# Edge search begun ahead of the small weights, its histogram counted in the same rounds, clears on two queues, last features split one group earlier

## The chip, the cores and the metric

One core of a Trainium2 chip. The metric is the device time of one execution in microseconds (us); the time before is the median of 3 runs. Engines: PE (TensorE), DVE (VectorE), ACT (ScalarE), POOL (GpSimd), SP (SyncE, which only issues DMAs here).

## What is computed

```python
edge_index = stack([src, dst])                       # 50000 edges, dst sorted, 3125 nodes, 256 features
# first layer, 3 hops:
msg = H[src...] * edge_weight                        # Hn = segment_sum(msg, rows) over the nodes
H = Hn @ Wn[i].T + bn[i] + H @ Ws[i].T + bs[i]       # elu after hops 0 and 1
x = layernorm(x + H)
# second layer, 8 heads of 32:
h = x @ W.T
alpha = leaky(h_src.a_src + h_dst.a_dst + sum(relu(edge_attr @ edge_W.T + edge_b) * h_dst))
attn = softmax of alpha over the edges of each dst
x = layernorm(x + segment_sum(h_src * attn, dst) + bias)
```

In the first layer `rows` is src and `cols` is dst.

## The kernel before, in words

The first layer multiplies by a dense adjacency of the graph that the kernel builds in HBM; the second works edge by edge on records sorted by dst. The kernel has these stages.

**Head.** SP loads edge ends, weights and attributes into tiles of 128 partitions x 392 edges (EC = 392), then the small weights (L444 to L449: b_cols, ew, a_cols, bias_b), x, and the weight matrices one after the other (L453, L467). Between the first matrix and the second stand 48 small copies of ew_parts into ew_j (L460, L463), which wait for parts that DVE makes in constants(). POOL clears the adjacency (10038528 words) with 18 DMAs of a zero tile, clear() at L411: 6 at once, 12 after some setup. DVE makes keys and cells of all edges in pair_cells(), and then the constants() that need the small weights.

**Search for equal pairs.** Two edges of one (dst, src) pair must be added up before they go to their cell. It runs in GROUPS = 49 rounds of U = 8 columns. For round t, DVE stages eight keys (kst, L1312), PE spreads them over all partitions (key_rows, L702), DVE compares them with the columns (find_pairs, L1323, eight compares of falling width, then to_cell L1327 and place L1330), PE adds the weights of equal pairs (pair_sums, L713, into a bank pair_totals(p)), and DVE reduces them to total (take_totals, L1334). POOL scatters each column with an adding indirect DMA (L578), 392 of them; it starts when all clears have landed, waits for the totals of each round, and for its own earlier scatters after each eight. In rounds 0 to 15 (UP = 16), PE takes four steps of first_products() after each round: transposes of the 7 weight matrices (L654), of x (L673), the first products (L643, L693). The other rounds are a hardware loop of two rounds per pass.

**Histogram of dst.** When the search is over, DVE splits the dst keys (L1353 to L1361, hi_d and lo_d), makes the one-hots of the window number, ohhi, for all 392 columns in seven instructions (L1372, over the tile of x_in), and then one low one-hot a round (ohlo, low_onehots, L1366) from which PE counts (count, L737, eight matmuls a round). Two ohlo buffers alternate. The histogram, copied at L1386, gives the start of each window's records.

**Ranks.** 49 rounds (PE rank_step L792, L799, spread L766, L777; ACT table copies; DVE ranks, L1426 to L1445) give the place of each edge in order of dst, place[:, 1].

**Hops.** SP waits for all scatters, places and table updates, then loads the adjacency in tiles a_t (L486). PE multiplies (L889) for 3 hops x 7 groups of 512 nodes (the last group, of 53, at L886), each over 25 windows. POOL meanwhile scatters the records by dst (L585), at times set by PE's progress, and reads them back (L590, s_dback). In hop 2 DVE does the layer norm of each group when its matmuls are done (L1513 residual, L1517, L1519, L1522), with means and variances on PE (L820, L826). Before the last group's residual, DVE calls split_features(), which splits the features of the records that were read back into three bf16 parts and makes the low keys (L1459 to L1477). PE then projects the last windows (L834), and the second layer begins.

The lines around the last split are these:

```python
for k in range(HOPS):
    for g in range(NG):
        if k == HOPS - 1 and g == NG - 1:
            split_features()
        ...
        if g < NG - 1:
            dve.wait_ge(s_amm, USED * (n + 1))
        else:
            dve.wait_ge(s_tail, 2 * HOPS)
```

Of the kernel before, what the change touches and what calls it, by code (L numbers as in the profile page):

```python
# [9 lines left out]
ALU = mybir.AluOpType  # L10
# [29 lines left out]
UP = 2 * U  # L40
# [43 lines left out]
def build(nc, x, src, dst, edge_attr, edge_weight, Wn, bn, Ws, bs, W, a_src, a_dst, edge_W, edge_b, bias, out):  # L84
    with ExitStack() as ctx:
# [88 lines left out]
        ohhiT = sb("ohhiT", [HI, U, P], F32, work)  # L174
        hist = sb("hist", [HI, LOK], F32, work)
# [78 lines left out]
        s_zero = sem("adjacency_cleared")  # L254
# [146 lines left out]
        def pair_totals(p):  # L401
            return bank[2 + p][:, 0:3 * U]
# [9 lines left out]
        def clear(eng, i):  # L412
            eng.dma_start(adj[i * P * FILL:(i + 1) * P * FILL, :].rearrange("(p c) o -> p (c o)", p=P),
                          zeros[:, :]).then_inc(s_zero, 16)
# [128 lines left out]
        def _(pool):  # L543
            pool.memset(identf[:, :], 0.0).then_inc(s_lane, 1)
            pool.wait_ge(s_blank, 5)
            for i in range(FILLS // 3):
                clear(pool, i)
# [17 lines left out]
            for i in range(FILLS // 3, FILLS):  # L565
                clear(pool, i)
# [3 lines left out]
            pool.wait_ge(s_zero, 16 * FILLS)  # L570
# [65 lines left out]
        def _(pe):  # L636
# [68 lines left out]
            def pair_sums(t, p, cold):  # L705
                pe.wait_ge(s_dup, U * t + U)
                if not cold:
                    pe.wait_ge(s_ptot, t - 1)
# [25 lines left out]
            def count(t, p, first, last=False):  # L734
                pe.wait_ge(s_lo, t + 1)
                for j in range(U):
                    i = pe.matmul(bank[1][0:HI, 0:LOK], ohhi[:, bass.ds(t * U + j, 1), :].rearrange("p c k -> p (c k)"),  # L737
                                  ohlo[:, p, j, :], start=first and j == 0, stop=last and j == U - 1, skip_group_check=True)
                i.then_inc(s_hist, 1)

            pe.wait_ge(s_hi, 7)
            pe.wait_ge(s_xT, len(ahead_x) + 2 * OWN_GROUPS)
            count(0, 0, True)
            count(1, 1, False)
            with pe.Fori(1, GROUPS // 2) as t:
                count(2 * t, 0, False)
                count(2 * t + 1, 1, False)
            count(GROUPS - 1, 0, False, True)
# [9 lines left out]
            def spread(t, s, n, cold):  # L758
                h, rows = bank[3 + s][0:HI, :], bank[5 + s]
                if cold:  # L760
                    pe.wait_ge(s_exc, 2)
                else:
# [251 lines left out]
        def _(act):  # L1014
# [8 lines left out]
            nc.scalar.copy(rec[:, 0:EC, 6], filled[:, :]).then_inc(s_rec, 1)  # L1023
            for m in range(2 * HOPS + 1):
# [10 lines left out]
            act.wait_ge(s_zero, 16 * FILLS)  # L1035
# [206 lines left out]
        def _(dve):  # L1242
# [66 lines left out]
            constants()  # L1309
# [31 lines left out]
            find_pairs(0, 0, True)  # L1341
            find_pairs(1, 1, True)
            take_totals(0, 0)
            with dve.Fori(1, GROUPS // 2) as t:
                find_pairs(2 * t, 0, False)
                take_totals(2 * t - 1, 1)
                find_pairs(2 * t + 1, 1, False)
                take_totals(2 * t, 0)
            find_pairs(GROUPS - 1, 0, False, True)
            take_totals(GROUPS - 2, 1)  # L1350
            take_totals(GROUPS - 1, 0)

            v.tensor_copy(dst_f[:, :], dst_i[:, :]).then_inc(s_hkey, 1)  # L1353
            v.tensor_scalar(cut_i[:, :], dst_i[:, :], SHIFT, None, ALU.logical_shift_right).then_inc(s_hkey, 1)
            v.tensor_scalar(group_i[:, :], dst_i[:, :], P - 1, None, ALU.bitwise_and).then_inc(s_hkey, 1)
# [430 lines left out]
```

## Time and profile before

| what | value |
|---|---|
| median of 3 runs | 3001.64 us (2999.54 to 3003.59) |
| the profiled execution, its own time | 3012.79 us |
| its span | 3011.0 us |
| mean granted TensorE clock | 0.786 |
| PE busy | 2305.8 us, 77% |
| POOL busy | 1634.0 us, 54% |
| DVE busy | 1471.4 us, 49% |
| ACT busy | 607.0 us, 20% |

The shares of busy time are means over stages with different limits. "Idle before" of a row is the time that its engine stood still before it, with what ended it. A line with an x count merges several instructions. Times of rows are microseconds from the start of the span.

### The profile page before, as it was taken

The page shows a single profiled execution, that of the slowest core. Times are in us where ns is not written, and L with a number is a line of the kernel's source. Part 1 is how long each engine was busy: PE and PEld are TensorE (multiplying, and loading weights), DVE is VectorE, ACT ScalarE, POOL GpSimd, SP SyncE. Part 2 cuts the span into 40 slices and gives each one's busy share as a digit, 9 for nine tenths or more (in the row PEclk, how much of TensorE's full clock was granted, in tenths as well). Part 3 has the DMA queues.
Part 4 walks back from the last instruction along what each step waited for, and adds up shares of the span by engine and source line. Part 5 has one row for each costly group of instructions (what it writes and reads, how often), then busy time and mean ns, then how long its engine had stood idle before and what let it go on. Part 6 is the DMA issues. An engine that isn't in the chain of part 4 may idle for free.

```text
span 3011.0 us, 40665 instructions
## 1 busy us (share of the span) xinstructions
PE 2305.8 (77%) x10293; PEld 1444.1 (48%) x10294; DVE 1471.4 (49%) x3883; ACT 607.0 (20%) x1667; POOL 1634.0 (54%) x1365
## 2 busy tenths in 40 slices
PE   0067443899999999999999999975566655664993
PEld 0055333577777644444444444444344443443772
DVE  2268999577777500000000111065565555667888
ACT  1021000022222100000001000012222222225994
POOL 1157777777777154444444442025555555545995
PEclk9987555555555699999999999987776677776997
DMA  9621221112121255444443445325555555554983
GB/s 382 239 22 1 0 0 0 0 1 0 0 0 0 69 148 144 131 116 139 133 136 108 136 131 163 113 81 169 171 156 165 161 163 162 164 155 143 270 267 113
DMA packets 297611, 350.47 MB, mean 116 GB/s; under 512 B 105434, under 2 KB 223921, under 8 KB 294961
## 3 DMA queue, kind: packets, MB, share of 16 engines
q1 hardware_dynamic: 205825, 247.70, 27.1%
q0 software_dynamic: 91696, 101.74, 16.5%
q8 instruction: 35, 0.57, 0.1%
q14 instruction: 55, 0.45, 0.0%
HBM read 242.39 MB, written 106.86 MB: 116 GB/s over the span
## 4 chain that ended last, share of the span: by engine, by line
PE 62%; issue 12%; DVE 11%; another core or an unknown queue 7%; SPq 4%; ACT 1%; DVEq 1%; DMA 0%; ACTq 0%; POOL 0%
PE psum L889 26%; PE psum L792 7%; PE psum L1006 7%; DVE found L1323 5%; PE psum L961 4%; PE psum L777 3%; SPq L447 2%; PE psum L799 2%; PE psum L737 2%; PE psum L643 2%; PE psum L878 2%; PE psum L766 1%; PE psum L952 1%; DVE acc L1557 1%
## 5 line engine op out<-in xcount | busy, mean ns | idle before, releaser
L578 POOL DMA_INDIRECT adjacency<-total,place x392 | 613.4, 1565 | 336.7 <-DVE total L1334 139.8
L585 POOL DMA_INDIRECT rows_by_dst<-rec,place x392 | 376.7, 961 | 501.4 <-PE psum L889 475.5
L599 POOL DMA_INDIRECT gath<-gat_rows,rec x416 | 398.5, 958 | 450.0 <-ACT digits L1186 183.3
L889 PE MATMUL psum<-a_t,acc 128*128 128x512 f32 x1200 | 527.1, 594 | 4.7 <-DMA a_t<-adjacency 4.7
L889 PEld LDWEIGHTS psum<-a_t,acc 128*128 128x128 f32 x1200 | 228.6, 191 | 275.3 <-issue 272.6
L961 PE MATMUL psum<-x,acc 128*128 x832 | 298.2, 510 | 65.7 <-DVE acc L1557 48.8
L1323 DVE SCALAR_TENSOR_TENSOR found<-psum,key_f,not_before 128x1024 bf16<-128x1024 f32 (+7 forms) x392 | 293.2, 815 | 0.1
L889 PE MATMUL psum<-a_t,x 128*128 128x512 f32 x600 | 262.2, 592 | 0.0
L961 PEld LDWEIGHTS psum<-x,acc 128*128 128x128 f32 x832 | 199.5, 257 | 130.2 <-issue 90.5
L1557 DVE TENSOR_TENSOR acc<-wT,psum 128x528 f32<-128x528 f32 x208 | 145.7, 700 | 220.4 <-issue 168.6
L792 PE MATMUL psum<-table,ohhiT 32*128 32x128 f32 x784 | 238.9, 457 | 0.3 <-ACT table L1065 0.3
L1006 PE MATMUL psum<-ht 128*128 128x264 f32 x832 | 210.8, 401 | 3.6 <-ACT ht L1214 3.6
L1498 DVE TENSOR_SCALAR et<-et 128x512 f32<-128x512 f32 (+1 forms) x28 | 11.6, 416 | 410.3 <-ACT et L1106 266.7
L615 POOL TENSOR_TENSOR ht<-gath,digits 128x1024 f32<-128x1024 f32 x104 | 198.1, 1913 | 18.1 <-ACT digits L1202 7.7
L792 PEld LDWEIGHTS psum<-table,ohhiT 32*128 32x128 f32 x784 | 181.1, 318 | 39.0 <-issue 21.6
L1169 ACT ACTIVATE wT<-psum 128x512 f32<-128x512 f32 x208 | 114.5, 596 | 418.8 <-remote 279.8
L1006 PEld LDWEIGHTS psum<-ht 128*128 128x128 f32 x832 | 152.4, 192 | 61.8 <-DVE x L1690 32.2
L702 PE MATMUL psum<-identf,kst 128*128 128x128 f32 x392 | 85.5, 392 | 124.7 <-DVE kst L1312 120.4
L889 PEld LDWEIGHTS psum<-a_t,x 128*128 128x128 f32 x600 | 113.9, 190 | 134.1 <-issue 133.0
L713 PE MATMUL psum<-w_parts,found 128*128 (+1 forms) x1764 | 59.9, 167 | 150.0 <-DVE found L1323 150.0
L928 PE MATMUL psum<-identb,lo_b 128*128 128x128 bf16 x420 | 64.1, 252 | 112.8 <-issue 81.0
L1426 DVE SCALAR_TENSOR_TENSOR terms<-psum,dst_f,earlier 128x128 f32<-128x128 f32 (+1 forms) x392 | 140.0, 414 | 10.9 <-DVE rank L1438 7.9
(282 smaller groups left out, 3018.2 us busy)
## 6 DMA issues: line engine op xcount, KB each, us to landing
a_t<-adjacency SPq DMA_DIRECT2D x450, 256.0 KB
gat_h_by_edge<-gath SPq DMA_DIRECT2D x104, 528.0 KB
gath<-gat_h_by_edge SPq DMA_DIRECT2D x104, 528.0 KB, 4.5
adjacency<-zeros POOLq DMA_DIRECT2D x18, 2178.5 KB, 48.3
gath<-gat_rows,rec POOLq DMA_INDIRECT x416
adjacency<-total,place POOLq DMA_INDIRECT x392
rows_by_dst<-rec,place POOLq DMA_INDIRECT x392
x_in<-in_x SPq DMA_DIRECT2D x1, 3072.0 KB
```

Source lines behind the costliest of these rows:

```text
L578: pool.indirect_dma_start(out=adj, in_=total[:, c:c + 1], out_offset=bass.IndirectOffsetOnAxis(ap=place[:, 0, c:c + 1], axis=0), in_offset ...
L585: pool.indirect_dma_start(out=rows_dst, in_=rec[:, c, :], out_offset=bass.IndirectOffsetOnAxis(ap=place[:, 1, c:c + 1], axis=0), in_offset ...
L599: pool.indirect_dma_start(out=gath[:, g % 4, c % 4, :], out_offset=None, in_=hh_dram, in_offset=bass.IndirectOffsetOnAxis(ap=rec_i[:, c, 0 ...
L615: nc.gpsimd.tensor_tensor(val[:, q, :, 0:D].rearrange("p c (h d) -> p c h d", h=HEADS), gath[:, q, :, 0:HX].rearrange("p c (h d) -> p c h ...
L792: pe.matmul(bank[7 * s][:, j * LOK:(j + 1) * LOK], ohhiT[:, 4 * s + j, :], table[:, half, :], start=True, stop=True, skip_group_check=True ...
L889: i = pe.matmul(sums[b], table_g[:, w, b * P:(b + 1) * P], a_t[:, q % NA, 0:width(g)], start=k == 0 and g < OWN_GROUPS and w == 0, stop=w ...
L961: i = pe.matmul(bank[4 + j][:, 0:HX], ohT[:, q % 2, j * P:(j + 1) * P], x0[:, bass.ds(ws[4 * (q % 2) + j], 1), :].rearrange("p c k -> p (c ...
L1006: pe.matmul(bank[4 * (q % 2) + j][:, 0:HX], onehot[:, q // 2, 4 * (q % 2) + j, :], val[:, q, j, :], start=True, stop=True).then_inc(s_mm, 1)
L1169: nc.scalar.activation(er[:, q % 2, 2 * p:2 * p + 2, :].rearrange("p c (h d) -> p (c h) d", d=HW)[:, :, 0:HD], bank[2 + p].rearrange("p (a ...
L1323: v.scalar_tensor_tensor(out=found[:, p, found_at(j):found_at(j) + n], in0=pair_rows(p)[:, j * P:U * P], scalar=key_f[:, bass.ds(t * U + j ...
L1426: v.scalar_tensor_tensor(out=terms[:, j, 0:wide], in0=bank[5 + q][:, j // 2 * 2 * P:j // 2 * 2 * P + wide], scalar=dst_f[:, bass.ds(t * U ...
L1557: v.tensor_tensor(prod[:, q % 2, 2 * p:2 * p + 2, :], er[:, q % 2, 2 * p:2 * p + 2, :], psum[:, (4 + 2 * p) * 512:(6 + 2 * p) * 512] .rear ...
```

## The change

- pair_cells() is followed at once by the split of the dst keys and by the first two rounds of the search; constants() comes after them.
- Each round of the search also makes a low one-hot (as before) and a window one-hot for its eight columns (the new tile ohhi_t, two buffers), and PE counts them after pair_sums, into bank 2. pair_totals has one bank instead of two, so pair_sums(t) waits for the totals of round t - 1 (before: t - 2). The seven ohhi instructions remain after the search, and the separate loop of the histogram is gone.
- first_products() is taken up in rounds 2 to 17 (UP = 18).
- 12 of the 18 clears are issued by ACT, after its copies into rec, with a semaphore of their own; POOL issues the first 6.
- split_features() is called one group sooner, before the residual of the last group but one.

```diff
-UP = 2 * U
+UP = 18
+        ohhi_t = sb("ohhi_t", [P, 2, U, HI], BF16, work)
         def pair_totals(p):
-            return bank[2 + p][:, 0:3 * U]
+            return bank[3][:, 0:3 * U]
# POOL
-            for i in range(FILLS // 3, FILLS):
-                clear(pool, i)
...
-            pool.wait_ge(s_zero, 16 * FILLS)
+            pool.wait_ge(s_zero, 16 * (FILLS // 3))
+            pool.wait_ge(s_zero2, 16 * (FILLS - FILLS // 3))
# ACT, after the copies into rec
+            act.wait_ge(s_blank, 5)
+            for i in range(FILLS // 3, FILLS):
+                clear(act, i, s_zero2)
# PE, pair_sums
                 if not cold:
-                    pe.wait_ge(s_ptot, t - 1)
+                    pe.wait_ge(s_ptot, t)
# PE
+            def count(t, p, first=False, last=False):
+                pe.wait_ge(s_lo, t + 1)
+                for j in range(U):
+                    i = pe.matmul(bank[2][0:HI, 0:LOK], ohhi_t[:, p, j, :], ohlo[:, p, j, :], start=first and j == 0,
+                                  stop=last and j == U - 1, skip_group_check=True)
+                i.then_inc(s_hist, 1)
             for t in range(UP):
                 key_rows(t + 1, (t + 1) % 2, t == 0)
-                pair_sums(t, t % 2, t < 2)
-                for _ in range(4):
-                    next(products, None)
+                pair_sums(t, t % 2, t == 0)
+                count(t, t % 2, t == 0)
+                if t >= 2:
+                    for _ in range(4):
+                        next(products, None)
...
-            with pe.Fori(U, GROUPS // 2) as t:
+            with pe.Fori(UP // 2, GROUPS // 2) as t:
                 key_rows(2 * t + 1, 1, False)
                 pair_sums(2 * t, 0, False)
+                count(2 * t, 0)
                 key_rows(2 * t + 2, 0, False)
                 pair_sums(2 * t + 1, 1, False)
+                count(2 * t + 1, 1)
             pair_sums(GROUPS - 1, 0, False)
+            count(GROUPS - 1, 0, False, True)
# DVE
             pair_cells()
-            constants()
+            v.tensor_copy(dst_f[:, :], dst_i[:, :]).then_inc(s_hkey, 1)
...
+            def count_onehots(t, p, cold):
+                if not cold:
+                    dve.wait_ge(s_hist, t - 1)
+                v.tensor_tensor(ohhi_t[:, p, :, :].rearrange("p c (a b) -> p c a b", b=2),
+                                hi_d[:, bass.ds(t * U, U), :].unsqueeze(2).broadcast_to([P, U, HI // 2, 2]),
+                                pairs_of(iota_b[:, 0:HI]).unsqueeze(1).broadcast_to([P, U, HI // 2, 2]),
+                                ALU.is_equal).then_inc(s_hi, 1)
+                low_onehots(t, p)
...
             find_pairs(0, 0, True)
+            count_onehots(0, 0, True)
             find_pairs(1, 1, True)
             take_totals(0, 0)
+            count_onehots(1, 1, True)
+            constants()
             with dve.Fori(1, GROUPS // 2) as t:
                 find_pairs(2 * t, 0, False)
                 take_totals(2 * t - 1, 1)
+                count_onehots(2 * t, 0, False)
...
             find_pairs(GROUPS - 1, 0, False, True)
             take_totals(GROUPS - 2, 1)
+            count_onehots(GROUPS - 1, 0, False)
             take_totals(GROUPS - 1, 0)
...
+            dve.wait_ge(s_hist, GROUPS)
             for c in range(0, EC, EC // 7):
...
-                    if k == HOPS - 1 and g == NG - 1:
+                    if k == HOPS - 1 and g == NG - 2:
                         split_features()
```

## Rows read from the trace of the kernel before

**Rows 1.** Busy time by stage: stretch, length, each engine, clock, DMA share, GB/s.

```profile
60.00:108.00 48.00, 0.00 (x0) 0.00 (x0) 0.00 (x0) 0.00 (x0) 0.00 (x0) 1.00 1.01 428
281.00:520.00 239.00, 105.00 (x1480) 90.56 (x1480) 218.66 (x666) 0.00 (x0) 180.08 (x117) 0.50 0.20 0
603.00:1027.00 424.00, 423.66 (x2343) 322.02 (x2341) 332.79 (x1219) 105.72 (x293) 279.38 (x179) 0.50 0.18 0
```

**Rows 2.** DMA issues of the page (first), then the timeline of the head: start, duration.

```profile
adjacency<-zeros POOLq DMA_DIRECT2D x18, 2178.5 KB, 48.3
...
24.81 0.49 DVE L380 CAST w_parts<-w_in 128x392 bf16<-128x392 f32 x1
...
46.52 63.98 SPq L447 DMA_DIRECT2D a_cols<-in_L_gnn_a_dst  x1
...
116.91 0.17 DVE L1294 TENSOR_TENSOR bcol<-b_cols 128x6 f32<-128x6 f32 x1 [90.94 <-DMA bias_b<-in_L_gnn_bias]
```

**Rows 3.** Timeline from 150 to 185 us: the stall for the second weight matrix.

```profile
156.92 1.11 PE L654 MATMUL psum<-identf,wraw 128*128 128x128 f32 x4 [26.57 <-DMA wraw<-in_L_gnn_Ws]
...
167.54 0.17 DVE L1312 COPY kst<-key_f 128x8 f32 x1 [32.51 <-PE psum L702]
...
183.41 0.21 DVE L1312 COPY kst<-key_f 128x8 f32 x1 [8.98 <-issue]
```

**Rows 4.** Timeline of the search: one round on PE, and to_cell of rounds 21 and 48.

```profile
317.88 1.33 PE L713 MATMUL psum<-w_parts,found 128*128 x36 [3.92 <-DVE found L1323]
...
319.10 1.97 PE L702 MATMUL psum<-identf,kst 128*128 128x128 f32 x8
...
324.69 0.17 DVE L1327 SCALAR_TENSOR_TENSOR to_cell<-left,cell 128x8 f32<-128x8 f32 x1
...
518.60 0.17 DVE L1327 SCALAR_TENSOR_TENSOR to_cell<-left,cell 128x8 f32<-128x8 f32 x1
```

**Rows 5.** Timeline of the keys, the window one-hots and the histogram.

```profile
520.35 0.35 DVE L1353 CAST dst_f<-dst_i 128x392 f32<-128x392 int32 x1
...
522.72 7.10 DVE L1372 TENSOR_TENSOR x_in<-hi_d,iota_b 128x1792 bf16<-128x1792 bf16 x7
529.74 1.29 DVE L1366 TENSOR_TENSOR ohlo<-lo_d,iota_b 128x1024 bf16<-128x1024 bf16 x2
...
590.42 2.42 PE L737 MATMUL psum<-ohlo,x_in 128*32 128x128 bf16 x16 [0.32 <-issue]
...
596.60 0.28 DVE L1386 COPY hist<-psum 32x128 f32<-32x128 f32 x1 [1.48 <-PE psum L737]
```

**Rows 6.** The scatter L578: its summary, then the timeline of GpSimd.

```profile
L578 POOL DMA_INDIRECT adjacency<-total,place x392: 1541/1542/2298, 135.9 to 971.1; - x196
...
175.17 1.54 POOL L578 DMA_INDIRECT adjacency<-total,place  x1 [26.50 <-DVE total L1334]
...
522.08 1.54 POOL L578 DMA_INDIRECT adjacency<-total,place  x1 [1.72 <-DMA adjacency<-total,place]
...
542.02 1.54 POOL L578 DMA_INDIRECT adjacency<-total,place  x1 [1.79 <-DMA adjacency<-total,place]
```

**Rows 7.** Timeline of SyncE's queue: the first loads of the adjacency.

```profile
1029.78 2.24 SPq L486 DMA_DIRECT2D a_t<-adjacency  x5
```

**Rows 8.** Timeline of the records read back and of the last groups of hop 2.

```profile
1852.68 0.60 POOL L590 DMA_DIRECT2D rec<-rows_by_dst  x1 [1.85 <-DMA rows_by_dst<-rec,place]
...
1961.67 1.41 DVE L1513 SCALAR_TENSOR_TENSOR zt<-psum,bcol,hcur 128x512 f32<-128x512 f32 x2 [29.17 <-PE psum L889]
...
1975.83 1.06 DVE L1459 COPY digits<-rec 128x1728 f32<-128x1728 f32 x1
...
1978.23 2.10 PE L834 MATMUL psum<-w1T,ht 128*128 128x272 f32 x8
...
1987.97 0.27 DVE L1513 SCALAR_TENSOR_TENSOR zt<-psum,bcol,hcur 128x53 f32<-128x53 f32 x1
...
1988.47 1.10 PE L820 MATMUL psum<-zt,mean_w 128*128 128x53 f32 x4 [8.14 <-DVE zt L1513]
```

More of the change, by code:

```diff
@@ L253, in build @@
         s_row = sem("keys_broadcast")
-        s_zero = sem("adjacency_cleared")
+        s_zero = sem("adjacency_cleared_by_gpsimd")
+        s_zero2 = sem("adjacency_cleared_by_scalar")
         s_later = sem("later_edges_marked")
@@ L410, in build, with clear @@
         G_BANK = (0, 4, 4)
-        def clear(eng, i):
+        def clear(eng, i, s_done):
             eng.dma_start(adj[i * P * FILL:(i + 1) * P * FILL, :].rearrange("(p c) o -> p (c o)", p=P),
-                          zeros[:, :]).then_inc(s_zero, 16)
+                          zeros[:, :]).then_inc(s_done, 16)
         ahead_x = [(w, min(2, USED - w)) for w in range(0, USED, 2)]
@@ L546, in _ @@
             for i in range(FILLS // 3):
-                clear(pool, i)
+                clear(pool, i, s_zero)
             pool.memset(ones[:, :], 1.0).then_inc(s_lane, 1)
@@ L761, in spread @@
                     pe.wait_ge(s_exc, 2)
+                    pe.wait_ge(s_hi, GROUPS + 7)
                 else:
@@ L1034, in _ @@
             act.wait_ge(s_fill, 2 + 16)
-            act.wait_ge(s_zero, 16 * FILLS)
+            act.wait_ge(s_zero, 16 * (FILLS // 3))
+            act.wait_ge(s_zero2, 16 * (FILLS - FILLS // 3))
             act.wait_ge(s_rec, 6)
@@ L1308, in _, with low_onehots @@
             pair_cells()
-            constants()
+            v.tensor_copy(dst_f[:, :], dst_i[:, :]).then_inc(s_hkey, 1)
+            v.tensor_scalar(cut_i[:, :], dst_i[:, :], SHIFT, None, ALU.logical_shift_right).then_inc(s_hkey, 1)
+            v.tensor_scalar(group_i[:, :], dst_i[:, :], P - 1, None, ALU.bitwise_and).then_inc(s_hkey, 1)
+            v.tensor_scalar(ident_w[:, :], identf[:, :], float(P), None, ALU.mult).then_inc(s_hkey, 1)
+            v.memset(earlier[:, 0:P], 1.0).then_inc(s_hkey, 1)
+            v.tensor_copy(earlier[:, P:2 * P], tri[:, :]).then_inc(s_hkey, 1)
+            dve.wait_ge(s_hkey, 6)
+            v.tensor_copy(hi_d[:, :, :], cut_i[:, :].unsqueeze(2).broadcast_to([P, EC, 2])).then_inc(s_hkey, 1)
+            v.tensor_copy(lo_d[:, :, :], group_i[:, :].unsqueeze(2).broadcast_to([P, EC, 2])).then_inc(s_hkey, 1)
+            dve.wait_ge(s_hkey, 8)
+            def low_onehots(t, p):
+                v.tensor_tensor(ohlo[:, p, :, :].rearrange("p c (a b) -> p c a b", b=2),
+                                lo_d[:, bass.ds(t * U, U), :].unsqueeze(2).broadcast_to([P, U, LOK // 2, 2]),
+                                pairs_of(iota_b[:, :]).unsqueeze(1).broadcast_to([P, U, LOK // 2, 2]),
+                                ALU.is_equal).then_inc(s_lo, 1)
+            def count_onehots(t, p, cold):
[6 more added lines that the diff above has]
+                low_onehots(t, p)
             def stage(t, p):
@@ L1375, in _ @@
                                 ALU.is_equal).then_inc(s_hi, 1)
-            low_onehots(0, 0)
-            low_onehots(1, 1)
-            with dve.Fori(1, GROUPS // 2) as t:
-                for p in range(2):
-                    dve.wait_ge(s_hist, 2 * t + p - 1)
-                    low_onehots(2 * t + p, p)
-            dve.wait_ge(s_hist, GROUPS - 2)
-            low_onehots(GROUPS - 1, 0)
             dve.wait_ge(s_hist, GROUPS)
-            v.tensor_copy(hist[:, :], bank[1][0:HI, 0:LOK]).then_inc(s_hd, 1)
-            v.tensor_reduce(in_window[:, 0:1], bank[1][0:HI, 0:LOK], X, ALU.add).then_inc(s_hd, 1)
+            v.tensor_copy(hist[:, :], bank[2][0:HI, 0:LOK]).then_inc(s_hd, 1)
+            v.tensor_reduce(in_window[:, 0:1], bank[2][0:HI, 0:LOK], X, ALU.add).then_inc(s_hd, 1)
             dve.wait_ge(s_hd, 2)
```

30 lines of the change are left out of this document (1 added, 29 removed).

## The prediction

> **What bounds the kernel now.** I read the busy time by stage first, then the timeline of the first 185 us, then one round of the search, the histogram, the scatter and the last group of the hops.
>
> The busy time by stage shows one engine at a time at its limit [rows 1]: from 60 to 108 us nothing but DMA works (the clears, 428 GB/s); from 281 to 520 us VectorE is busy 218.66 of 239 us in the search; from 603 to 1027 us TensorE is busy 423.66 of 424 us in the ranks.
>
> The head [rows 2]: the weights of the edges are split at 25 us, and the search could start, but VectorE sits in constants() (L1294) for 90.94 us, until 116.91, for the small weights. Those stand behind SyncE's a_cols load, whose issue alone took 63.98 us beside the 18 clears of 2178.5 KB and ended at 110.54.
>
> Then a second stall [rows 3]: TensorE waits 26.57 us for the second weight matrix, which SyncE issues only after the 48 small ew_j copies; round 2's kst comes at 167.54, after 32.51 us of idle VectorE, and round 3's at 183.41.
>
> From there VectorE sets the pace [rows 4]: to_cell of round 21 starts at 324.69, of round 48 at 518.60, so 193.91 / 27 = 7.18 us a round. TensorE has for a round pair sums of 1.33 us and key rows of 1.97 us, and waits.
>
> After the search [rows 5] come the split of the dst keys (520.35 to 522.72, 2.37 us), seven window one-hots (7.10 us), and the histogram, a ping-pong of one low one-hot and eight matmuls (L737, 2.42 us for two rounds' sixteen), from 529.74 to 596.60: 66.86 us.
>
> GpSimd's 392 scatters run from 135.9 to 971.1 us, the eighth at 175.17 [rows 6]: 795.9 / 384 = 2.07 us each, 16.58 us a round. The first a_t load is issued at 1029.78 [rows 7], released by the ranks, so the scatter has about 57 us to spare.
>
> **The change, part by part** (against the profiled execution, 3012.79 us, whose span is 3011.0).
>
> *Start of the search.* Two rounds and their one-hots run from about 28 to 45 us, then VectorE stands in constants() as before. What follows is the old schedule with the round number raised by two: first_products() is taken up in round 2 now, the ew_j loads and weight loads stand behind the same waits, so the round after the stall starts at 167.5 as before, but is round 4. Gain: 2 x 7.18 = 14.4 us. I cost the two early rounds at nothing: the clears cover them, with some 70 us to spare.
>
> *Histogram in the rounds.* Removed from the path: 66.86 us and, as the dst keys are split under the clears, 2.37 us. Added to VectorE in each round: one low one-hot and one window one-hot of 256 elements. The low one is 1.29 / 2 = 0.65 us, the wide one of 1792 elements 7.10 / 7 = 1.01 us [rows 5]; that is 0.48 ns an element, so 256 elements cost 0.65 - 768 x 0.48 ns = 0.28 us. With 0.05 us (my estimate) for the extra wait, 0.97 us a round. It counts in rounds 5 to 48, 44 of them, as rounds 0 to 4 lie under the clears or the weight stall: 42.7 us. Bounds: 0.65 us a round, if the smaller one vanishes in VectorE's loop gap, and 1.25 us, if no instruction overlaps the next: 29 to 55 us. I take the value from the rows of the same operation.
>
> TensorE adds half of 2.42, 1.21 us: with 1.33 and 1.97 it has 4.5 us of work in a round of 8.15 us. The single bank for totals makes pair sums wait for the totals of the round before, 0.5 us after the search of a round; nothing needs those sums for another 7 us. In the product rounds the longer VectorE round takes in about 1 us of TensorE's lateness: -1 us. At the end the window one-hots wait for the last count (pair sums, then 1.21 us): +1.3 us. The seven window one-hots stay on the path, 7.1 us.
>
> *Clears from two queues.* The bytes are the same and the 16 DMA engines already full [rows 1], so the end of the clears does not move: 0. ScalarE issues its twelve after its copies, and its next work is the first weight matrix, past 129 us: 0. The small loads share the DMA engines with two queues of large rows instead of one for some time and may keep more work for after the clears. After a_cols was issued (110.54) the rest took until 116.91 [rows 2], 6.4 us; I add half of it, 3 us, to the whole chain. Bounds: 0 and 14 us, the latter being all that the two early rounds bring.
> The Trainium skill (DMA: Bandwidth & Descriptors, Queues, rings and completion order) says that each DMA engine takes turns between the queues that have work. By that the small loads' share falls from a half to a third while both clear queues are active, which speaks for the 3 us and against 0; the trace, with one clear queue, cannot show it.
>
> *Scatter.* It still waits, at 175.17 [rows 6], for the first totals made after the weight stall, but with 23 columns done there instead of 7: it ends 2 x 16.58 = 33 us sooner, near 938 us, against ranks that end near 990: hidden, 50 us to spare.
>
> *Last features split sooner.* The records are read back from 1852.68 on; split_features() (1975.83 to 1987.97) now runs while VectorE idles 29.17 us for the matmuls of the sixth group [rows 8], so it costs nothing there: 12.1 us into 29. The last group's residual no longer stands behind it. TensorE idled 8.14 us for that residual at 1988.47; it has its projections until 1980.33, so its mean matmuls start there: 8.1 us gained. All that follows (variances, projections, stored rows, gathers) hangs on this chain. Were the cover gone, the 12.1 us would be paid one group earlier.
>
> *Sum.* 14.4 + 66.9 + 2.4 - 42.7 + 1 - 1.3 - 3 + 8.1 = 45.8, so -46 us: 2967 for a profiled execution like this one. The median of the runs shown, 3001.64, is 11.15 below it; less 46 it is 2956.
>
> **The rivals.**
>
> 1. The small loads come much later (ScalarE's clears crowd them or end later). Then the gain of the two rounds is gone, whatever they did. For it: a_cols took 64 us beside one clear queue. Against it: the bytes do not change. The bound of 14 us instead of the 3 us taken is 11 us more: 2967.
> 2. The split brings nothing, because another wait takes the residual's place. For it: TensorE and ScalarE go hand in hand there. Against it: the row names VectorE's residual as what ended TensorE's idle time. 8 us less: 2964.
> 3. Slower: the one-hots in every round hold up GpSimd's scatters, until these release the hops. Eight scatters took 19.94 us (522.08 to 542.02) while the seven window one-hots ran [rows 6], against 16.58. Were every round so, 47 rounds x 3.36 = 158 us, the scatter would end at 1096 instead of 1028, +68 - 8 = +60: 3062. It decides from 18.7 us a round, where the hops start as much later as the split gives back. Against it: in that stretch one-hots ran without a break for 7 us; in the new round they run 0.9 of 8.2 us.
> The Trainium skill (GPSIMD Engine Reference, Key points) says that GpSimd shares its SBUF interfaces with VectorE and contends with VectorE instructions of two SBUF inputs, which these compares are. It speaks for rival 3; the stretch from 522.08 agrees in kind.
> 4. Slower: the round grows past 9.2 us (2 us added instead of 0.97), say by VectorE waiting for key rows that now stand behind the count. 44 x 1.04 us more eats the whole gain. TensorE's 4.5 us of work a round speaks against it; at 10 us a round it would be 3037.
> 5. The change doesn't do what it says: the search does not get going before 117 us, and the one-hots cost their upper bound: 14 and 12 us less, 2982.
>
> **How the numbers follow.** Forecast 0.68, rival 1 0.13, rival 2 0.07, rival 3 0.04, rival 4 0.03, rival 5 0.05. The range goes from 2942 (0.65 us a round, -14) to 2974 (one-hots at 1.25 us a round, +12, with a few us of later weights); rivals 1 and 2 lie in it. This kernel's measurement can tell about 0.2% (6 us) from no change. Faster 0.92, within 0.2% 0.01, slower 0.07.
>
> **What would show it.** Two rounds of L1323 before 50 us; the wait at L1294 still ending near 117 to 120; rounds of 8.15 us between two to_cells; the copy of the histogram near 559 instead of 596.60; the first a_t load near 992; GpSimd's last scatter near 940; no idle TensorE before the last mean matmuls. I am wrong if the wait at L1294 ends past 125, if a round is above 8.5 us or below 7.8, or if a DMA of the adjacency, not the ranks, releases the first a_t load.

## The result and the profile after

| what | before | after |
|---|---|---|
| median, same chip | 3000.59 us (2996.74 to 3003.59, 4 runs) | 2927.64 us (2922.92 to 2931.55, 4 runs) |
| ratio | | 0.9753 (0.9738 to 0.9767) |
| the profiled execution, its own time | 3012.79 us | 2922.92 us |
| its span | 3011.0 us | 2921.2 us |
| mean granted TensorE clock | 0.786 | 0.806 |
| DVE busy | 1471.4 us | 1474.3 us |

The kernel is 73 us faster; I had forecast 46, and at most 60. Timed again (e0, beside a kernel before of 3016.28 us) it gave 0.9767 (0.9746 to 0.9787). The ratio of e5 further down leaves out one disturbed execution, of 7169 us.

Busy time by stage, after (stretch, length, busy time of PE, of its weight loads PEld, of DVE, ACT and POOL, granted TensorE clock with 1.00 for 2.4 GHz, DMA share, GB/s), for [rows 1]: the search from round 5 to round 48, and the ranks.

```profile
189.24:518.41 329.17, 203.99 (x2390) 168.86 (x2390) 315.51 (x945) 19.07 (x41) 247.82 (x159) 0.65 0.20 1
528.16:961.40 433.24, 427.80 (x2358) 323.72 (x2358) 338.65 (x1240) 106.33 (x295) 312.44 (x200) 0.50 0.19 0
```

The bounds are those of before: VectorE in the search, TensorE in the ranks. The head, from the page (ScalarE's clears; the other six are GpSimd's) and the timeline (start, duration, engine, line), for [rows 2, 3]: the to_cells are those of rounds 1, 3, 4 and 5.

```profile
adjacency<-zeros ACTq DMA_DIRECT2D x12, 2178.5 KB, 57.3
...
43.21 0.17 DVE L1354 SCALAR_TENSOR_TENSOR to_cell<-left,cell 128x8 f32<-128x8 f32 x1
65.73 44.40 SPq L449 DMA_DIRECT2D a_cols<-in_L_gnn_a_dst  x1
116.79 0.17 DVE L1297 TENSOR_TENSOR bcol<-b_cols 128x6 f32<-128x6 f32 x1 [71.78 <-DMA bias_b<-in_L_gnn_bias]
133.76 0.17 DVE L1354 SCALAR_TENSOR_TENSOR to_cell<-left,cell 128x8 f32<-128x8 f32 x1
173.52 0.17 DVE L1354 SCALAR_TENSOR_TENSOR to_cell<-left,cell 128x8 f32<-128x8 f32 x1
189.24 0.17 DVE L1354 SCALAR_TENSOR_TENSOR to_cell<-left,cell 128x8 f32<-128x8 f32 x1
```

The weight matrix still holds the search until 167 us, and it is round 4 that stands behind it. The wait for the small weights ends where it did, at 116.79. One round of the search on DVE, for [rows 4]:

```profile
306.17 0.17 DVE L1354 SCALAR_TENSOR_TENSOR to_cell<-left,cell 128x8 f32<-128x8 f32 x1
306.60 0.18 DVE L1361 TENSOR_REDUCE total<-psum 128x24 f32 x1
306.75 0.29 DVE L1332 TENSOR_TENSOR ohhi_t<-hi_d,iota_b 128x256 bf16<-128x256 bf16 x1
306.96 0.68 DVE L1324 TENSOR_TENSOR ohlo<-lo_d,iota_b 128x1024 bf16<-128x1024 bf16 x1
307.56 0.16 DVE L1339 COPY kst<-key_f 128x8 f32 x1
313.75 0.17 DVE L1354 SCALAR_TENSOR_TENSOR to_cell<-left,cell 128x8 f32<-128x8 f32 x1
```

A round is 7.58 us, against 7.20 of before at this place (7.02 and 7.38 in turn). The eight count matmuls take TensorE 1.03 us of it. The last to_cell, the copy of the histogram (the seven window one-hots, still 7.10 us, lie between them) and the first a_t load, then the scatter, for [rows 5 to 7]:

```profile
518.41 0.17 DVE L1354 SCALAR_TENSOR_TENSOR to_cell<-left,cell 128x8 f32<-128x8 f32 x1
528.16 0.27 DVE L1395 COPY hist<-psum 32x128 f32<-32x128 f32 x1
961.40 0.81 SPq L488 DMA_DIRECT2D a_t<-adjacency  x2
```
```profile
L579 POOL DMA_INDIRECT adjacency<-total,place x392: 1541/1542/2257, 112.1 to 938.7; - x196
...
957.97 1.23 PE psum L791 x4
```

The second fence is the scatter's summary and the chain's last piece ahead of that load: TensorE's rank matmuls, so the ranks release the hops, not the scatter. Last, the last groups of hop 2 (timeline, then windows of TensorE from the last mean matmuls to the stored rows, first after, then before), for [rows 8]:

```profile
1893.07 1.41 DVE L1522 SCALAR_TENSOR_TENSOR zt<-psum,bcol,hcur 128x512 f32<-128x512 f32 x2 [17.00 <-PE psum L888]
1911.95 1.15 PE L833 MATMUL psum<-w1T,ht 128*128 128x272 f32 x4
...
1911.00:1917.10 6.10, 4.68 (x25) 3.31 (x23) 3.46 (x8) 3.37 (x17) 0.00 (x0) 1.00 0.00 1
```
```profile
1989.36 2.14 PE L834 MATMUL psum<-w1T,ht 128*128 128x272 f32 x4
...
1988.00:1997.00 9.00, 7.90 (x24) 6.00 (x25) 3.87 (x12) 2.59 (x13) 0.00 (x0) 0.57 0.01 3
```

Where the time went, by the two traces:

| stretch | before | after | gain | forecast |
|---|---|---|---|---|
| to_cell of before's round 3, after's round 5 | 189.66 | 189.24 | 0.4 | -3 (small loads) |
| the two rounds not done after it (before, 504.84 to 518.60) | | | 13.8 | 14.4 |
| the same 43 rounds | 315.2 | 329.2 | -14.0 | -41.7 (one-hots, stalls) |
| last to_cell to the copy of the histogram | 78.0 | 9.75 | 68.2 | 68.0 |
| last full group's residual to the last stored rows | 35.3 | 23.9 | 11.4 | 8.1 |

Together 80 us up to the last stored rows (1996.94 to 1916.93). The profiled execution of before was itself 12 us above its median, and that of after 5 us below. What stands behind the stored rows, the second layer, was 10 us shorter in the profile of after, but by the medians it must have been some 7 us longer (80 less 73), or 11.5 by e0 (80 less 68.5). From first to last gather it took 699.6 us in the profile of before and between 679.9 and 708.8 in those of after and of e0 to e7, e10 and e11, none of which touches it. Whether 7 to 11.5 us of the 80 are really given back there is open: it is less than this spread.

### The profile page after: what moved, and what is told of

Read it like the earlier page. It is cut to its first block, busy times and chain, and to the rows that moved or that the text cites. A ratio compares the mean times of both kernels' runs of the same rounds, so it can differ in the third digit from the quotient of the medians.

```text
span 2921.2 us, 40192 instructions
## 1 busy us (share of the span) xinstructions
PE 2272.8 (78%) x10293; PEld 1425.5 (49%) x10294; DVE 1474.3 (50%) x3932; ACT 606.9 (21%) x1667; POOL 1629.3 (56%) x1353
## 4 chain that ended last, share of the span: by engine, by line
PE 64%; issue 12%; DVE 11%; another core or an unknown queue 6%; SPq 5%; ACT 1%; DVEq 1%; DMA 1%; ACTq 0%; POOL 0%
PE psum L888 27%; PE psum L791 8%; PE psum L1005 7%; PE psum L960 5%; DVE found L1350 5%; PE psum L776 3%; PE psum L798 2%; PE psum L877 2%; PE psum L644 2%; SPq L449 2%; PE psum L951 2%; PE psum L765 1%; PE psum L927 1%; SPq L446 1%
## 5 line engine op out<-in xcount | busy, mean ns | idle before, releaser
L579 POOL DMA_INDIRECT adjacency<-total,place x392 | 613.9, 1566 | 310.1 <-issue 112.1
L960 PE MATMUL psum<-x,acc 128*128 x832 | 292.3, 502 | 74.2 <-DVE acc L1566 45.9
L714 PEld LDWEIGHTS psum<-w_parts,found 128*128 128x128 bf16 x1764 | 55.9, 103 | 229.9 <-issue 229.3
```

The costliest lines, as they stand in the source:

```text
L579: pool.indirect_dma_start(out=adj, in_=total[:, c:c + 1], out_offset=bass.IndirectOffsetOnAxis(ap=place[:, 0, c:c + 1], axis=0), in_offset ...
L714: i = pe.matmul(pair_totals(p)[:, 3 * f:3 * f + 3], found[:, p, at:at + P], w_parts[:, bass.ds(t * U + j, 1), :].rearrange("p c k -> p (c ...
L960: i = pe.matmul(bank[4 + j][:, 0:HX], ohT[:, q % 2, j * P:(j + 1) * P], x0[:, bass.ds(ws[4 * (q % 2) + j], 1), :].rearrange("p c k -> p (c ...
```

## The experiments

e1 to e4 and, in a second session, e0, e6, e7 and e10 ran on one chip (the kernel before took 3016.89 and 3016.28 us there), e5 and e11 on a second (2998.66), e9 and e12 on a third (2828.68). The kernel before was timed beside each. On the third chip every kernel takes about 170 us less; in the traces of e9 and e12 this lies behind the stored rows, where the gathers took 526 us instead of about 700.

**The two rounds.** Theory: they were won by TensorE's first products being taken up two rounds later, so that four rounds instead of two are done before the weight stall; beginning ahead of the small weights is worth nothing by itself. Rival, and what the prediction said: the early start brought them.

e3_constants_first:

```diff
             pair_cells()
+            constants()
...
-            constants()
```

> The changed kernel with constants() put back ahead of the search, first_products() still taken up from round 2. Theory A (the two rounds are won because the first products, which block TensorE until the weight matrices come, are taken up two rounds later; where the search starts does not matter, as two more rounds fit into the stall for the weights between 135 and 166 us): the copy of the histogram stays within 2 us of 528.16 and the time within 3 us of the changed kernel. Rival B (the prediction's: they are won because the search starts under the clears): the copy of the histogram comes near 543, and the time is 15 us longer.

2946.4 us, ratio 0.9759 (0.9736 to 0.9782). The timeline of DVE, round 3, and SyncE's first load:

```profile
152.60 0.17 DVE L1355 SCALAR_TENSOR_TENSOR to_cell<-left,cell 128x8 f32<-128x8 f32 x1
...
962.32 1.76 SPq L488 DMA_DIRECT2D a_t<-adjacency  x4
```

With the search begun only after the small weights, four rounds end by 153 us, before the matrix comes (round 4's to_cell follows at 173.92), and the first load is 0.9 us later than in the changed kernel. The early start was worth 1 us.

e6_products_two_rounds_later, the converse, on the kernel before:

```diff
-UP = 2 * U
+UP = 18
...
-                for _ in range(4):
-                    next(products, None)
+                if t >= 2:
+                    for _ in range(4):
+                        next(products, None)
-            with pe.Fori(U, GROUPS // 2) as t:
+            with pe.Fori(UP // 2, GROUPS // 2) as t:
```

> The kernel before, with nothing changed but that the first products are taken up from round 2 instead of round 0. The search still starts after the small weights. Theory A (the two rounds were won by what lies in the weight stall, not by starting ahead of the small weights): rounds 0 to 3 have ended before the stall, the copy of the histogram comes at about 582 us instead of 596.60, the first a_t load at about 1015 instead of 1029.78, and the time is 14 to 15 us shorter. Theory B (the early start was what brought them): rounds 2 and 3 push the stall back by their own length, nothing moves, 0 to 3 us.

3002.16 us against 3016.28, ratio 0.9959 (0.9945 to 0.9974).

```profile
148.48 0.17 DVE L1328 SCALAR_TENSOR_TENSOR to_cell<-left,cell 128x8 f32<-128x8 f32 x1
...
1010.81 1.29 SPq L486 DMA_DIRECT2D a_t<-adjacency  x3
```

Round 3's to_cell stands at 148.48, round 4's at 173.56, the copy of the histogram at 577.64, and all that follows is a good 16 us sooner than in e7, which is the kernel before up to the hops (1027.41), 14 by the medians. Three small edits bring the whole gain of the moved search (theory A).

e9_products_two_rounds_later_again carries it on in the changed kernel:

```diff
-UP = 18
+UP = 20
...
-                if t >= 2:
+                if t >= 4:
```

> The changed kernel with the first products taken up from round 4 instead of round 2, and nothing else. Theory A (every round that can be done before TensorE turns to the products, whose second weight matrix comes at about 167 us, saves its full length): rounds 4 and 5 start at about 141 and 149 us, the first a_t load comes two rounds sooner, at about 946 instead of 961, the scatter (it ends near 938) still hidden; 15 us less than the changed kernel, ratio near 0.972. Theory B (with 6 rounds the gap is full and the products come late by what is put ahead of them): 0 to 5 us.

2737.17 us, 91.5 below the kernel before on its chip (68.5 and 73 for the changed kernel in e0 and in the result), ratio 0.9678 (0.9662 to 0.9695). Round 5, and the first load:

```profile
148.93 0.17 DVE L1355 SCALAR_TENSOR_TENSOR to_cell<-left,cell 128x8 f32<-128x8 f32 x1
...
946.55 0.82 SPq L489 DMA_DIRECT2D a_t<-adjacency  x2
```

961.40 - 946.55 = 14.9 us for two rounds: six are done before the stall instead of four.

e10_eight_rounds_ahead goes to the end of it, and here eight rounds are done ahead of the small weights:

```diff
-UP = 18
+UP = 28
+AHEAD = 8
...
-                if t >= 2:
+                if t >= 12:
...
             constants()
-            with dve.Fori(1, GROUPS // 2) as t:
+            with dve.Fori(AHEAD // 2, GROUPS // 2) as t:
```

(and rounds 2 to 7 written out ahead of constants()).

> The changed kernel with eight rounds of the search ahead of the constants instead of two, and the first products taken up from round 12 instead of round 2. Theory A (each round that lies before the weight stall saves its 7.58 us, until the scatter bounds the hops: 392 calls from 112 us at 2.08 us end at about 928): ten more rounds would bring 76 us, the scatter allows 33; the first a_t load comes at about 928, released by the scatter, and the time is about 33 us below that of the changed kernel (ratio near 0.964). Theory B (the small weights or TensorE's products do not move with it, as the rounds push them back): less than 10 us, or slower.

2911.0 us (2908.36 to 2914.49) against 2947.76 of the changed kernel beside it; ratio to before 0.9647 (0.963 to 0.9665). It is faster than both. The chain of waits (the last scatter and its landing), then TensorE:

```profile
928.29 3.04 DMA adjacency<-total,place
...
934.10 1.19 PE L889 MATMUL psum<-a_t,acc 128*128 128x512 f32 x1 [39.65 <-DMA a_t<-adjacency]
```

The bound has moved: the last scatter, at 928.29, releases the hops, and TensorE stands idle for 39.65 us. Ten more rounds were worth 30 us of the first load (931.35 instead of 961.40; 37 us by the medians); the rest waits for GpSimd's 392 calls. What the early start adds to this is not shown, as no run takes the products up that late without it. My estimate from the times above: between the end of constants() (about 120 us) and the second weight matrix (about 166) there is room for six rounds of 7.6 us, and e9 has six done by then. So only what e10 gains on e9, 946.55 - 931.35 = 15.2 us, can need the early start.

**The histogram.** Theory: a round has idle time of VectorE between the totals and the next keys, and the one-hots fill it first. Rival (the prediction): 0.97 us a round is paid in full.

e4_histogram_after takes the one-hots and counts out of the rounds into a loop behind the search:

```diff
                 key_rows(2 * t + 1, 1, False)
                 pair_sums(2 * t, 0, False)
-                count(2 * t, 0)
...
             count_onehots(GROUPS - 1, 0, False)    # and all others, now here:
+            count_onehots(0, 0, True)
+            count_onehots(1, 1, True)
+            with dve.Fori(1, GROUPS // 2) as t:
+                count_onehots(2 * t, 0, False)
+                count_onehots(2 * t + 1, 1, False)
```

> The changed kernel with the one-hots and counts of the histogram taken out of the search rounds and run as a loop of their own after the search, all else as changed. Theory A (each round of the search keeps about half a microsecond in which VectorE waits for its own loop and copies, and the one-hots, 0.9 us of work, fill it, so they add 0.40 us a round): the round falls from 7.58 to 7.18 us, the last to_cell comes some 18 us before 518.41, the histogram loop then takes 67 to 70 us, and the time is about 50 us longer. Rival B (the growth of the round from 7.18 to 7.58 comes from the single bank for totals and the one-hots are free): the round stays at 7.58, and the time is 67 us longer. Rival C (the prediction's cost of 0.97 us a round, with something else in the change making rounds faster): the round falls to 6.6 us and the time is about 25 us longer.

2969.92 us, ratio 0.9846 (0.9825 to 0.9866), 24 above e3. The last to_cell comes at 503.44, so rounds cost 15 us less in all, and the loop takes from 505.24 to 549.68. Two rounds of the search, then the loop in windows (columns as above) and the copy:

```profile
302.48 0.17 DVE L1356 SCALAR_TENSOR_TENSOR to_cell<-left,cell 128x8 f32<-128x8 f32 x1
309.50 0.17 DVE L1356 SCALAR_TENSOR_TENSOR to_cell<-left,cell 128x8 f32<-128x8 f32 x1
316.88 0.17 DVE L1356 SCALAR_TENSOR_TENSOR to_cell<-left,cell 128x8 f32<-128x8 f32 x1
...
506.00:549.00 43.00, 31.14 (x385) 22.79 (x386) 41.13 (x97) 0.00 (x0) 32.93 (x20) 0.95 0.19 0
...
556.70 0.27 DVE L1398 COPY hist<-psum 32x128 f32<-32x128 f32 x1
```

A round takes 7.02 and 7.38 us in turn, as in the kernel before, although the totals still have one bank. So the bank costs nothing that can be seen (rival B is out), and the one-hots with their counts add 7.58 - 7.20 = 0.38 us to a round, as theory A says; rival C's 6.6 us is out too. The copy is 28.5 us later than in the changed kernel. Theory A expected about 50, and there it was wrong: the separate loop, although VectorE now also makes the window one-hots in it, takes 44.4 us instead of 66.9. The reason for that took two more runs.

How the 0.4 us comes about is seen from starts on VectorE. In the kernel before, kst starts 0.33 and 0.72 us after the totals in turn, though VectorE has nothing else to do and no wait for another engine is named:

```profile
303.71 0.18 DVE L1334 TENSOR_REDUCE total<-psum 128x24 f32 x1
304.04 0.21 DVE L1312 COPY kst<-key_f 128x8 f32 x1
...
310.70 0.18 DVE L1334 TENSOR_REDUCE total<-psum 128x24 f32 x1
311.42 0.17 DVE L1312 COPY kst<-key_f 128x8 f32 x1 [0.53 <-issue]
```

After, the distance is 0.95 to 1.00 us in the steady rounds, here 0.96 (306.60 to 307.56): 0.15 for the totals, 0.21 and 0.60 for the one-hots. Before it is 0.53 in the mean. So of the 0.81 us of one-hots only 0.96 - 0.53 = 0.43 us is added (the round grew by 0.38 to 0.40), and 0.38 us vanish in what VectorE left empty behind the totals (0.53 less their own 0.15). What fills that empty time in the kernel before is not shown; the row calls it issue. e5_one_more_onehot asks whether the next one is free too:

```diff
                 low_onehots(t, p)
+                v.tensor_tensor(extra[...], lo_d[...], pairs_of(iota_b[...]), ALU.is_equal)   # 128x1024
```

> The changed kernel with a second low one-hot (128x1024, 0.68 us) into a tile of its own in each round of the search. Theory A (the first 0.5 us that are added to a round vanish in VectorE's gap between the totals and the next keys, what comes after that is paid in full): the gap is used up already, so each round grows by about 0.63 us, from 7.58 to 8.2, 45 rounds are 28 us, the copy of the histogram comes near 556 instead of 528, ratio near 0.986. Theory B (VectorE's added compares overlap with other work at a constant share, 0.40 us paid of 0.97): 0.26 us a round, 7.85, the copy near 540, ratio near 0.980.

Ratio 0.9839 (0.9815 to 0.9863), 25 us above 0.9753 of a 2999 us kernel.

```profile
411.27 0.17 DVE L1362 SCALAR_TENSOR_TENSOR to_cell<-left,cell 128x8 f32<-128x8 f32 x1
412.66 0.68 DVE L1341 TENSOR_TENSOR extra<-lo_d,iota_b 128x1024 bf16<-128x1024 bf16 x1
413.26 0.16 DVE L1347 COPY kst<-key_f 128x8 f32 x1
419.45 0.17 DVE L1362 SCALAR_TENSOR_TENSOR to_cell<-left,cell 128x8 f32<-128x8 f32 x1
```

8.18 us a round, 0.60 more, in full (412.66 to 413.26); the copy of the histogram comes at 551.78. The first piece is cheap, the next is not: theory A, rather than a constant share.

**The old loop.** e11_idle_before_histogram puts the seven window one-hots, in which TensorE idles, ahead of e4's loop, as in the kernel before:

```diff
+            for c in range(0, EC, EC // 7):
+                v.tensor_tensor(ohhi[:, c:c + EC // 7, :]...)
             count_onehots(0, 0, True)
             count_onehots(1, 1, True)
```

> The histogram in a loop of its own after the search, as in the run with the histogram after, but with the seven window one-hots (7.1 us, in which TensorE has nothing to do) ahead of the loop and not behind it; the slices that TensorE reads stay the static ones. Theory A (the loop of the kernel before took 67 us as TensorE entered it after 9 us of idling and stayed at 1.2 GHz): the loop takes 60 to 67 us, the granted clock in it is 0.50, the copy of the histogram comes near 573. Theory B (what made the old loop slow was TensorE reading a column chosen by a register): the clock rises within some 5 us, the loop takes 45 to 48 us, the copy comes near 556 as before the edit.

e12_column_by_register is e11 with one difference (and the wait for the seven one-hots that it needs):

```diff
-                    i = pe.matmul(bank[2][0:HI, 0:LOK], ohhi_t[:, p, j, :], ohlo[:, p, j, :], ...)
+                    i = pe.matmul(bank[2][0:HI, 0:LOK], ohhi[:, bass.ds(t * U + j, 1), :]..., ohlo[:, p, j, :], ...)
```

> The run with TensorE idle ahead of the histogram, with one difference: TensorE takes the window one-hot of each column from the tile of all columns, at a column chosen by a register, as the kernel before did, and no longer from the small tile of two rounds. VectorE does the same work. Theory A (reading by a register is what made the old loop slow): sixteen matmuls take 2.4 to 2.5 us instead of 1.9 at 1.2 GHz, the granted clock stays at 0.50, the loop takes 60 to 67 us instead of 45, the copy of the histogram comes near 573. Theory B (it is something else in the old loop, such as its hand-over between two buffers): the loop stays at 45 to 50 us, the copy comes near 556 to 560.

e11: ratio 0.9829 (0.98 to 0.9857). e12: 0.9908 (0.9892 to 0.9925). Summary of line L722 (ns min/median/max), windows behind the idle time, and the copy, for e11 and then e12:

```profile
L722 PE MATMUL psum<-ohlo,ohhi_t x392: 219/219/314, 512.0 to 555.6; 128*32 128x128 bf16 x196
...
512.00:522.00 10.00, 8.32 (x82) 6.51 (x83) 8.75 (x21) 0.00 (x0) 8.48 (x6) 0.69 0.20 0
522.00:540.00 18.00, 12.92 (x168) 9.26 (x167) 17.53 (x42) 0.00 (x0) 14.22 (x9) 1.00 0.20 0
...
555.90 0.28 DVE L1398 COPY hist<-psum 32x128 f32<-32x128 f32 x1 [0.78 <-PE psum L722]
```
```profile
L722 PE MATMUL psum<-ohlo,x_in x392: 265/283/314, 511.7 to 577.2; 128*32 128x128 bf16 x196
...
522.00:540.00 18.00, 15.94 (x107) 10.74 (x107) 11.65 (x27) 0.00 (x0) 13.93 (x9) 0.50 0.18 0
...
577.60 0.28 DVE L1400 COPY hist<-psum 32x128 f32<-32x128 f32 x1 [1.33 <-PE psum L722]
```

Both enter the loop after 8.1 to 8.2 us without a matmul. With static slices the granted clock goes to 2.4 GHz and the copy comes at 555.90; with the register it stays at 1.2 GHz and the copy comes at 577.60, with 1.37 us a round as in [rows 5]. So theory A of e11 (the idle time ahead) is refuted, and theory A of e12 (the register) holds. The two ran on different chips, with their last to_cell at 502.24 and 501.87.

e12 also reads another tile than e11. That this is not the reason stands in its own trace: its first two rounds are written out, so their columns are fixed, and they read the same tile.

```profile
511.70 1.86 PE L722 MATMUL psum<-ohlo,x_in 128*32 128x128 bf16 x16 [8.18 <-DVE ohlo L1328]
...
516.65 2.41 PE L722 MATMUL psum<-ohlo,x_in 128*32 128x128 bf16 x16 [0.32 <-issue]
```

Sixteen matmuls take 1.86 us with fixed columns and 2.41 with the register, both at 1.2 GHz. At least 21.7 us of the old histogram's 66.9 came from this way of reading, not from the work; at least, because in e11 VectorE is busy 17.53 of 18 us and sets the pace in TensorE's stead.

**The split.** Theory: besides TensorE's 8.1 us of idle time, the change removes what that idle time did to the clock. Rival: 8.1 us and no more.

e7_split_sooner_alone, on the kernel before:

```diff
-                    if k == HOPS - 1 and g == NG - 1:
+                    if k == HOPS - 1 and g == NG - 2:
                         split_features()
```

> The kernel before, with nothing changed but that the last features are split one group sooner. Theory A (the split's 12 us off the path remove TensorE's 8.1 us of idle time and, as its clock then stays at 2.4 GHz, another 3.3 us of its projections and means): the stretch from the last full group's residual to the last stored rows shrinks from 34.9 us to 23.5, and the time by about 11 us. Theory B (my prediction): 8.1 us, the stretch ends at about 27 us and the projections still take 2.1 us each.

3002.84 us, ratio 0.9957 (0.9944 to 0.9971), 13 us with some 4 either way. The window over the stretch, then one row of PE's timeline:

```profile
1959.50:1983.20 23.70, 22.40 (x93) 12.66 (x92) 10.68 (x16) 5.20 (x18) 0.00 (x0) 1.00 0.17 43
...
1978.65 1.15 PE L834 MATMUL psum<-w1T,ht 128*128 128x272 f32 x4
```

The last rows are stored at 1983.64, 23.9 us behind the residual instead of 35.3.

e1_split_late is the converse on the changed kernel (the split back at the last group):

> The changed kernel with split_features() put back ahead of the last group's residual. Theory A (the early split gives back VectorE's delay of 8.1 us and, as TensorE does not stand still, its clock does not fall to the lower level in the matmuls behind it, 3.3 us more): the stretch from the last full group's residual to the last stored rows grows from 23.4 to about 34.9 us, the granted clock in the last 9 us of it is near 0.57 instead of 1.00, and the time is 11.4 us longer. Rival B (the delay alone): 8.1 us longer, clock unchanged.

2950.89 us, ratio 0.9779 (0.9756 to 0.9802), 4.5 us above e2 and e3, with intervals that overlap. The medians alone can't tell 11.4 us from 8.1, or from nothing; the trace can:

```profile
1920.63 1.10 PE L819 MATMUL psum<-zt,mean_w 128*128 128x53 f32 x4 [8.13 <-DVE zt L1522]
...
1919.00:1928.00 9.00, 7.21 (x20) 5.56 (x20) 5.04 (x14) 1.71 (x8) 0.00 (x0) 0.53 0.00 1
```

The idle 8.13 us is back, and with it a granted clock of 0.53 behind it and four projections in 2.14 us instead of 1.15. The rows are stored at 1928.82, 35.0 us behind the residual, against 23.9 in e3: 11.1 us more, where theory A said 11.4 and the rival 8.1.

**The clears.** e2_clears_gpsimd issues all 18 from GpSimd again:

```diff
+            for i in range(FILLS // 3, FILLS):
+                clear(pool, i, s_zero2)
...
-            for i in range(FILLS // 3, FILLS):
-                clear(act, i, s_zero2)
```

> The changed kernel with all 18 clears issued by GpSimd again. Theory A (the DMA engines are full, the queue does not matter): the wait for the small weights in constants() ends within 1 us of 116.79, the scatter starts near 112, and the time is the same within 3 us. Rival B (the two clear queues hold up the small loads, as the prediction took): the wait ends 3 us sooner than with two queues, and the time is 3 us shorter.

2946.33 us, ratio 0.9758 (0.9736 to 0.978).

```profile
117.46 0.17 DVE L1296 TENSOR_TENSOR bcol<-b_cols 128x6 f32<-128x6 f32 x1 [72.40 <-DMA bias_b<-in_L_gnn_bias]
```

The wait for the small weights ends 0.7 us later with one queue. The second queue neither brings nor costs anything that can be measured.

e0_after_again is the changed kernel itself, timed beside e6, e7 and e10:

> The changed kernel unaltered, timed on the chip of the three beside it, so that they have something to be held against. Both theories: ratio 0.973 to 0.977 to the kernel before, first a_t load at 961 us, rounds of 7.58 us.

2947.76 us, ratio 0.9767 (0.9746 to 0.9787), first load at 961.57.

## Why the prediction was right and wrong

Right in direction, wrong in size: 73 us (ratio 0.9753) against a forecast of 46 and a range that ended at 60.

- **Histogram in the rounds, the added part: the step that failed.** "0.97 us a round", "44 of them", 42.7 us; measured 0.40 us a round, and 14.0 us over the rounds behind the stall, once the 3 us that the longer round took out of the products' stalls are in it. This one term holds 27.7 of the 34 us by which the traced stretches were missed (41.7 against 14.0 in the table). Of the 0.97, 0.38 us vanish in the time that VectorE left empty between the totals and kst. My lower bound, 0.65, let only the small one-hot vanish in "VectorE's loop gap", 0.28 us by its row; the gap takes 0.38 of whatever stands there, and I had it in the trace: kst came 0.33 and 0.72 us after totals that nothing separated from it. Another 0.16 us were no cost at all: the durations, 0.28 and 0.65, where the next instruction starts 0.21 and 0.60 us on, and the 0.05 for the extra wait.
- **The removed histogram** (66.9, 2.4 and -1.3 us): 68.2 measured, as forecast. What the row did not tell was that a third of it came from reading a column by register, and that part could be had without moving the histogram: in e4 the loop took 44.4 us.
- **Start of the search.** 14.4 us forecast, 13.8 measured, but for a reason that the text only half had. It said that the products are "taken up in round 2 now" and credited the two early rounds; e3 and e6 show that the take-up alone does it, and that the room for two more rounds lay behind the small weights, in the weight stall.
- **Clears and small loads.** -3 us forecast with bounds of 0 and 14; measured 0.1 (116.91 to 116.79), and e2 0.7. The lower bound was right. The Trainium skill (DMA: Bandwidth & Descriptors, Queues, rings and completion order) says that an engine takes turns among the queues with work; from that I had argued for the 3 us. The rows of SyncE's queue agree with it: with two clear queues the last three b_cols loads took 30.19 us to issue and ew 14.80, against 17.61 and 7.86 before, and 17.62 and 7.87 in e2. But what they lost did not reach the end: a_cols began 19 us later, and its issue still ended at 110.13, against 110.50, when the clears were done. The step from slower small loads to 3 us at the end was the wrong one.
- **Split.** The mechanism is right and its 8.1 us are in e1's row; the term lacked the 3.3 us that the clock at 1.2 GHz added to the projections behind the idle time. The row of a four-matmul group at 2.14 us, beside 2.10 for eight just before, was there to be read.
- **Rivals.** 1 and 2 did not come. 3 (one-hots hold up the scatters): the 24th scatter starts at 174.88, the last at 938.7, so 763.8 / 368 = 2.076 us each against 2.073 before; the mean call is 1566 ns against 1565. The Trainium skill (GPSIMD Engine Reference, Key points) names contention of GpSimd with two-input VectorE instructions on SBUF; where such compares run without a break the traces agree: during the seven window one-hots of after, two calls took 2.26 and 2.19 us instead of 1.54, and in e4's loop some took 2.04. In the rounds, with 0.81 us of them in 7.58, the mean call took 1.56 us (247.57 / 159) against 1.54 (180.08 / 117), and the pace did not suffer. 4: the round is 7.58 us, not 9.2. 5: the search does start at 28 us. No rival made the change faster than the forecast. With the one-hots at their forecast price the stretches would have gained 80 - 27.7 = 52 us, inside the range.
- **What would show it.** Two rounds before 50 us, the wait at 116.79, the last scatter at 938.7 and no idle time before the last mean matmuls stood as written. The round, 7.58, fell below the 7.8 that I had named as the sign of being wrong; the copy came at 528.16, not 559, and the load at 961.40, not 992.

Open: why the traces gain 80 us up to the stored rows and the medians 73 and 68.5 in all; why the clock rises in e11 and not in e12; and what keeps VectorE from starting kst sooner behind the totals.

## What to carry to other kernels

Price an added instruction by the distance between starts, and first look for what the engine already leaves empty at that place: here the first 0.38 us were free, and the next one-hot was paid in full. When a part moves ahead of a wait, ask which later wait it then fits in front of; here the gain came from the order of TensorE's work, could be had in a few lines without the rest, and went on (e9, e10) until the scatter was the bound. Idle time of TensorE can cost more than itself when matmuls follow it closely: here 11.4 us for 8.1.

## What was unexpected of the hardware

- Sixteen matmuls that read one operand at a column chosen by a register took 2.41 to 2.42 us at 1.2 GHz ([rows 5], e12), those with a fixed one 1.86 to 1.93 us (e4, e11, the first two rounds of e12). The clock stayed at 1.2 GHz for the whole loop of 66 us with the register (TensorE busy 15.94 of 18 us), and rose to 2.4 GHz within its first 10 us without.
- Behind 8.1 us of idle time the granted clock was 0.57 (before) and 0.53 (e1) over the last 9 us before the stored rows, and the same work took 3.3 us less where that idle time was gone.
- The keys' copy started 0.33 or 0.72 us after the totals in turn, with nothing between them on VectorE but the totals' own 0.15; added work of 0.81 us there lengthened the round by 0.38 to 0.40, and another 0.60 us by 0.60 (e5).
- Indirect DMA calls of GpSimd took up to 2.26 us instead of 1.54 while VectorE ran compares of two SBUF tiles without a break (after, 519 to 528 us), and kept 1.56 in the mean where such compares fill 0.81 of 7.58 us.
